# Two transformer-like blocks on images, third stage: the second product runs eleven strips behind the first, its scale is made over three steps, the residual has three buffers, and the loop is written out

## The reference

```python
x = _L0_conv_ref(x, ...)   # shifted 7x7 window attention, then an MLP of 192 hidden units
x = _L1_conv_ref(x, ...)   # the second block:
y = conv7x7_depthwise(x) + dw_b
y = layernorm_over_channels(y)
y = gelu(y @ w1.T + b1)                      # 48 -> 192 features per pixel
gx = sqrt(sum over all pixels of y * y)      # one number per image and feature
nx = gx / (mean of gx over the features + 1e-6)
y = grn_g * (y * nx) + grn_b + y
out = x + (y @ w2.T + b2)                    # 192 -> 48
```

## Time and profile before

| | before |
|---|---|
| runs, us | 2073.83 median of 3 (2071.69 to 2075.19) |
| the profiled execution, us | 2077.34 |
| its span, us | 2075.7 |
| mean granted TensorE clock | 0.946 of full |
| busy: PE, DVE, ACT, POOL | 86%, 73%, 75%, 57% of the span |
| first r_OUT of the response phase starts at | 1734.3 us |
| last r_OUT (strip 63) starts at | 2060.2 us |

### The profile page before, as it was taken

How to read it: one execution, slowest core, us unless ns; L and a number is a source line. 1 busy time by engine, 2 the same in 40 slices (tenths; PEclk the granted TensorE clock), 3 DMA queues, 4 the chain that set the end, 5 groups by cost and what they waited for, 6 DMA issues and landing times. The chain is left out here.

```text
span 2075.7 us, 90932 instructions
## 1 busy us (share of the span) xinstructions
PE 1777.1 (86%) x38074; PEld 1065.6 (51%) x38074; DVE 1508.5 (73%) x2014; ACT 1550.2 (75%) x2882; POOL 1174.7 (57%) x1048
## 2 busy tenths in 40 slices
PE   4989898989888898989898989874999959889884
PEld 2655555555555555555555555531788823223321
DVE  7687777878777777787777777534777757767772
ACT  3788888888888888888888888763566658777770
POOL 4676767777776767676767777731455611111121
PEclk9999999999999999999999999985899957889998
DMA  4334544343434343434434343312587769899983
GB/s 106 80 101 106 146 104 115 91 115 87 119 84 118 86 118 87 109 96 105 100 97 109 93 112 83 93 32 56 155 216 211 203 128 197 218 217 211 242 200 105
DMA packets 233223, 262.18 MB, mean 126 GB/s; under 512 B 167078, under 2 KB 179910, under 8 KB 232710
## 3 DMA queue, kind: packets, MB, share of 16 engines
q1 hardware_dynamic: 217478, 217.50, 43.1%
q0 software_dynamic: 15360, 39.08, 6.6%
HBM read 160.82 MB, written 80.88 MB: 116 GB/s over the span
## 5 line engine op out<-in xcount | busy, mean ns | idle before, releaser
L415 POOL TENSOR_TENSOR shift<-const_b,qmax 113x588 bf16<-113x588 bf16 x256 | 345.8, 1351 | 55.1 <-DVE qmax L510 54.9
L440 POOL TENSOR_TENSOR xl<-x 113x784 bf16<-113x784 f32 x64 | 136.7, 2136 | 263.8 <-DVE x L532 263.8
L1475 POOL DMA_DIRECT2D out_rolled<-r_OUT x128 | 64.3, 504 | 319.5 <-DVE r_OUT L1577 316.4
L510 DVE TENSOR_REDUCE qmax<-ps_s 113x12 f32<-113x588 f32 x256 | 194.7, 760 | 63.0 <-PE ps_s L890 63.0
L496 DVE TENSOR_TENSOR xh<-X,RS 113x784 f32<-113x784 f32 x64 | 229.1, 3580 | 2.9 <-DMA RS<-rs_scratch 2.1
L731 ACT ACTIVATE G<-ps_m 128x392 f32<-128x392 f32 x384 | 184.1, 498 | 50.9 <-PE ps_m L992 50.1
L699 ACT ACTIVATE P<-ps_t 113x588 f32<-113x588 f32 x256 | 171.9, 672 | 54.2 <-PE ps_t L942 53.5
L1323 PE MATMUL conv_ps<-xin,band_now 64*64 64x448 bf16 x2688 | 203.1, 364 | 4.1 <-DVE x_low L1225 4.1
L405 POOL TENSOR_TENSOR xhl<-xh 113x784 bf16<-113x784 f32 x64 | 203.4, 3178 | 2.2 <-DVE xh L550 2.2
L692 ACT COPY Uf<-ps_m 113x392 f32<-113x392 f32 x384 | 172.8, 485 | 30.9 <-PE ps_m L857 22.6
L502 DVE TENSOR_TENSOR Ul<-Uf 113x784 bf16<-113x784 f32 x192 | 182.6, 977 | 0.0
(11 more groups left out here) (240 smaller groups left out, 5267.3 us busy)
## 6 DMA issues: line engine op xcount, KB each, us to landing
xin<-rows_scratch SPq DMA_DIRECT2D x96, 236.0 KB, 3.8
XT<-x_tokens SPq DMA_DIRECT2D x64, 294.0 KB, 4.6
X<-x_windows SPq DMA_DIRECT2D x128, 147.0 KB, 2.9
RS<-rs_scratch SPq DMA_DIRECT2D x128, 147.0 KB, 3.4
XR<-x_windows SPq DMA_DIRECT2D x128, 147.0 KB, 3.7
x_scratch<-x SPq DMA_DIRECT2D x128, 147.0 KB, 3.9
y_scratch<-y POOLq DMA_DIRECT2D x96, 196.0 KB, 2.8
r_RS<-rs_scratch SPq DMA_DIRECT2D x128, 147.0 KB, 3.8
```

Of the source, the lines that this page charges most:

```text
L415: nc.gpsimd.tensor_tensor(shift[:, j % 2], e, m, ALU.mult).then_inc(S["md"], 1)
L440: nc.gpsimd.tensor_tensor(xl1[:], x1[:, r, :], x1m[0][:, r, :], ALU.subtract).then_inc(S["x1_lo"], 1)
L510: nc.vector.tensor_reduce(qmax[:, j % 2, :].rearrange("p (b n) -> p b n", b=2), ps_s[0:R, :, 0:2 * HQ].rearrange("p b (n t) -> p b n t", t ...
```

## The change

The second product, r_OUT and the stores run 11 steps behind the first product in place of 10 (`LAG`), with 14 buffers of features in place of 16 (`RING`); the per-strip sums keep 16 places (`SLOTS`). The making of the scale is taken apart. With B the first step after an image's last strip (strip B-8 is the image's first): in step B, DVE makes r_total, PE adds the halves between its first products of tiles 1 and 2, and ACT takes the square root after the Gelu of tile 2; in step B+1, PE makes the mean of the norms, again between tiles 1 and 2, and ACT (no longer DVE) adds epsilon to it with an Identity and a bias; in step B+2, DVE makes the scale and the scaled weights behind r_OUT; in step B+3, PE uses them. The small products go to spare columns of r_ps_m, and the first product of tile 2 waits until they have been read. On DVE the sum of squares follows its strip by one step in place of two. r_X has three buffers and is loaded one step ahead of its use, at the head of SP's step in place of its end. The hardware loop is gone: all steps are written out.

```diff
--- before.py
+++ after.py
@@ -1377,8 +1377,10 @@
...
         N = strips
-        RING = 2 * STRIPS
-        LAG = STRIPS + 2
+        RING = STRIPS + 6
+        SLOTS = 2 * STRIPS
+        LAG = STRIPS + 3
+        XRING = 3
         by_strip = [t.rearrange("b c (g s n) -> b s g c n", g=2, s=STRIPS) for t in (x2_dram, out_dram)]
@@ -1391,7 +1393,7 @@
...
         Y = sb("r_Y", [R, 2, STRIP])
-        X2 = sb("r_X2", [ROWB + C, 2, STRIP])
+        X2 = sb("r_X2", [ROWB + C, XRING, STRIP])
         OUT = sb("r_OUT", [ROWB + C, 2, STRIP])
@@ -1401,10 +1403,11 @@
...
         junk_act = sb("r_junk_act", [128, 2, STRIP])
-        sums = sb("r_sums", [128, 2, RING])
+        sums = sb("r_sums", [128, 2, SLOTS])
         total = sb("r_total", [128, 2])
...
         mean = sb("r_mean", [128, 1])
+        eps1 = sb("r_eps1", [128, 1])
         inv = sb("r_inv", [128, 1])
@@ -1412,9 +1415,9 @@
...
         S = sems("cleared y_cleared setup_v setup_t f1 f2 pairs mean_ps xh summed summed_act totals "
-                 "gx_made inv_made scaled w2_scaled out_made ge lo")
+                 "gx_made mean_made inv_made scaled w2_scaled out_made ge lo")
         y_loaded = [sem(f"r_y_loaded{r}") for r in range(2)]
-        x2_loaded = [sem(f"r_x2_loaded{r}") for r in range(2)]
+        x2_loaded = [sem(f"r_x2_loaded{r}") for r in range(XRING)]
         stored = [sem(f"r_stored{r}") for r in range(2)]
@@ -1424,16 +1427,9 @@
...
-        def steps(eng, step, last):
-            turns = max((N - RING - 2) // RING, 0)
-            for raw in range(-2, RING):
-                step(Strip(0, raw, N))
-            if turns:
-                with eng.Fori(0, turns) as i:
-                    for u in range(RING):
-                        step(Strip(RING // 4 * i, RING + u, N))
-            for raw in range(RING + RING * turns, last):
+        def steps(step, last):
+            for raw in range(-2, last):
                 step(Strip(0, raw, N))
@@ -1442,7 +1438,15 @@
...
             def step(s):
-                nxt, old = s.at(2), s.at(-LAG)
+                nxt, old = s.at(2), s.at(1 - LAG)
+                if old.real:
+                    if old.n == 0:
+                        wait(sp, S["cleared"], CLEARS)
+                    wait(sp, S["out_made"], old.n - XRING + 1)
+                    for g in range(2):
+                        sp.dma_start(X2[ROWB * g:ROWB * g + C, old.slot(XRING), :],
+                                     by_strip[0][old.n // STRIPS, old.n % STRIPS, g]
+                                     ).then_inc(x2_loaded[old.slot(XRING)], 16)
                 if nxt.real:
@@ -1452,16 +1456,8 @@
...
                                      ).then_inc(y_loaded[r], 16)
-                if old.real:
-                    if isinstance(old.n, int) and old.n == 0:
-                        wait(sp, S["cleared"], CLEARS)
-                    wait(sp, S["out_made"], old.n - 1)
-                    for g in range(2):
-                        sp.dma_start(X2[ROWB * g:ROWB * g + C, old.slot(2), :],
-                                     by_strip[0][old.n // STRIPS, old.n % STRIPS, g]
-                                     ).then_inc(x2_loaded[old.slot(2)], 16)
-            steps(sp, step, N + LAG)
+            steps(step, N + LAG)
@@ -1478,7 +1474,7 @@
...
-            steps(pool, step, N + LAG)
+            steps(step, N + LAG)
             for r in range(2):
@@ -1493,6 +1489,7 @@
...
                 nc.vector.memset(t[:], 1.0).then_inc(S["y_cleared"], 1)
+            nc.vector.memset(eps1[:], EPS1).then_inc(S["y_cleared"], 1)
             dve.wait_ge(S["cleared"], CLEARS)
@@ -1529,19 +1526,17 @@
...
                     wait(dve, S["ge"], 3 * s.n + 3)
-                    g = G[:, s.raw % RING, 2, :]
+                    g, at = G[:, s.raw % RING, 2, :], s.raw % SLOTS
                     wait(dve, S["summed"], s.n)
                     nc.vector.tensor_tensor_reduce(out=junk[:], in0=g, in1=g, scale=1.0, scalar=0.0, op0=ALU.mult,
-                                                   op1=ALU.add, accum_out=sums[:, 1, s.raw % RING:s.raw % RING + 1]
+                                                   op1=ALU.add, accum_out=sums[:, 1, at:at + 1]
                                                    ).then_inc(S["summed"], 1)
-            def image(s):
-                return s.raw // STRIPS if isinstance(s.i, int) else s.i // 2 + s.raw // STRIPS
             def add_up(s):
...
                 if s.real and s.raw % STRIPS == 0:
-                    img, p = image(s), s.raw // STRIPS % 2
+                    img, p = s.raw // STRIPS, s.raw // STRIPS % 2
+                    wait(dve, S["pairs"], img)
                     wait(dve, S["summed"], s.n + STRIPS)
@@ -1550,13 +1545,12 @@
...
                 if s.real and s.raw % STRIPS == 0:
-                    img, p = image(s), s.raw // STRIPS % 2
-                    wait(dve, S["mean_ps"], img + 1)
-                    nc.vector.tensor_scalar(mean[:], ps_o[:, 0, HALF + 2:HALF + 3], EPS1, None, ALU.add
-                                            ).then_inc(S["inv_made"], 1)
-                    wait(dve, S["inv_made"], 2 * img + 1)
+                    img, p = s.raw // STRIPS, s.raw // STRIPS % 2
+                    wait(dve, S["mean_made"], img + 1)
+                    wait(dve, S["scaled"], 2 * img)
                     nc.vector.reciprocal(inv[:], mean[:]).then_inc(S["inv_made"], 1)
-                    wait(dve, S["inv_made"], 2 * img + 2)
+                    wait(dve, S["inv_made"], img + 1)
+                    wait(dve, S["w2_scaled"], 2 * img)
                     nc.vector.scalar_tensor_tensor(out=scale[:], in0=gx[:], scalar=inv[:, 0:1], in1=grn_g[:],
@@ -1571,35 +1565,36 @@
...
                     n = ROWB + C
-                    wait(dve, x2_loaded[s.slot(2)], 32 * (s.turn(2) + 1))
+                    wait(dve, x2_loaded[s.slot(XRING)], 32 * (s.raw // XRING + 1))
                     wait(dve, stored[s.slot(2)], 32 * s.turn(2))
...
                         out=halves(OUT[:, s.slot(2), :]), in0=ps_o[0:n, :, 0:HALF], scalar=out_b[:, 0:1],
-                        in1=halves(X2[:, s.slot(2), :]), op0=ALU.add, op1=ALU.add).then_inc(S["out_made"], 1)
+                        in1=halves(X2[:, s.slot(XRING), :]), op0=ALU.add, op1=ALU.add).then_inc(S["out_made"], 1)
...
                 nx2 = s.at(2)
-                respond(s.at(-LAG))
-                sum_squares(s.at(-2))
-                add_up(s.at(-LAG + 1))
+                sum_squares(s.at(-1))
+                add_up(s.at(-STRIPS))
                 finish(s.at(-LAG))
+                respond(s.at(-STRIPS - 2))
                 normalise(nx2)
-            steps(dve, step, N + LAG)
+            steps(step, N + LAG)
...
             act.wait_ge(S["cleared"], CLEARS)
+            act.wait_ge(S["y_cleared"], 3)
...
                     wait(act, S["summed_act"], s.n)
-                    slot = s.raw % RING
+                    slot, at = s.raw % RING, s.raw % SLOTS
                     nc.scalar.activation(junk_act[:], G[:, slot, 0:2, :], ACT.Square,
-                                         accum_out=sums[:, 0, slot:slot + 1]).then_inc(S["summed_act"], 1)
+                                         accum_out=sums[:, 0, at:at + 1]).then_inc(S["summed_act"], 1)
@@ -1615,18 +1610,30 @@
...
                 if s.real and s.raw % STRIPS == 0:
-                    img = s.raw // STRIPS if isinstance(s.i, int) else s.i // 2 + s.raw // STRIPS
+                    img = s.raw // STRIPS
                     wait(act, S["pairs"], img + 1)
-                    nc.scalar.activation(gx[:], ps_o[:, 0, HALF:HALF + 2], ACT.Sqrt).then_inc(S["gx_made"], 1)
+                    wait(act, S["scaled"], 2 * img)
+                    wait(act, S["mean_ps"], img)
+                    nc.scalar.activation(gx[:], ps_m[:, 0, HALF:HALF + 2], ACT.Sqrt).then_inc(S["gx_made"], 1)
+            def keep_mean(s):
+                if s.real and s.raw % STRIPS == 0:
+                    img = s.raw // STRIPS
+                    wait(act, S["mean_ps"], img + 1)
+                    wait(act, S["inv_made"], img)
+                    nc.scalar.activation(mean[:], ps_m[:, 0, HALF + 2:HALF + 3], ACT.Identity, bias=eps1[:, 0:1]
+                                         ).then_inc(S["mean_made"], 1)
...
                 features(s, 1)
-                norms_root(s.at(-LAG + 1))
                 features(s, 2)
+                keep_mean(s.at(-STRIPS - 1))
+                norms_root(s.at(-STRIPS))
                 sum_squares(s)
-            steps(act, step, N + LAG)
+            steps(step, N + LAG)
@@ -1652,9 +1659,10 @@
...
                         wait(pe, S["lo"], s.n + 1)
-                        wait(pe, S["ge"], 3 * (s.n - 1) + 1)
-                    elif t == 1:
-                        wait(pe, S["ge"], 3 * s.n)
+                    wait(pe, S["ge"], 3 * (s.n - 1) + t + 1)
+                    if t == 2 and s.raw >= STRIPS:
```

(41 more changed lines are left out.)

## The result

The changed kernel takes 2040.1 us (median of 4 runs, 2038.1 to 2042.9) against 2072.8 (median of 4, 2071.4 to 2075.2): ratio 0.984, 95% interval 0.9825 to 0.9859, so 33 us less. The forecast was 2038, 36 less. The profiled execution has a span of 2038.6 us in place of 2075.7.

A forecast was written before the change was run, and what follows sets the result against it. Taken as bounds: r_OUT's waits for r_X and the chain at image boundaries with its low clock. Start +4.9, six images -32.9, end -8.2 sum to -36.2; against 2073.8 that gave 2038 us, range 2026 to 2062.

The forecast's parts named there:

- The residual: Response phase: r_OUT's wait for r_X falls from 36.4 us to under 3; r_Y is late next.
- the tens of us that were to be a sign of being wrong: Sign against the prediction: r_xh waiting for r_Y by tens of us, where it waited 4.6 us before.
- An ordinary strip: Strips between boundaries: 4.16 us at PE's pace where buffers are full, 4.65 in three of eight, 1.5 us an image.
- The boundary: Between two images: 1.0 small products, 1.25 PE waiting for Gelu, 0.7 for the weights; 3.0 us over eight bare strips.
- The clock: TensorE in the response phase: stays up at boundaries, 1.00 through the middle, where a boundary had 0.51.
- The rival with 2.5 us in each image: Clock still falls at each image boundary, costing 2.5 us an image: 2053 us, chance 0.15.
- An image: Eight strips and a boundary: 33.3 + 3.0 + 1.5 = 37.8 us, -32.9 us over six images.
- The start and the end: r_OUT of strip 0 starts 4.9 us later; strips 48 to 63 take 58.1 us, -8.2.
- The loop: All steps written out in place of the hardware loop: 0, bounded at 10 us gained or lost.
- The tables: ACT at boundaries: two loads of 1.28 us without drain, at most 16; rival of Identity needing its own: 2058, chance 0.04.
- PE's pace throughout: Rival, response phase: DMA share over 1 is not full, an image takes 36.3 us: 2029 us, chance 0.12.
- The transfer engines as the bound: Rival: all eight strips at 4.65 us, an image 40.2, +14.4: 2052 us, chance 0.18.

The follow-up runs named there:

- the fastest kernel: Changed kernel with three buffers for r_Y, r_RS and r_OUT, second product ahead of tile 0 except at an image's first strip, scale before sum of squares: 2027.9 us, ratio 0.9771.
- The mixed order: Changed kernel, second product ahead of tile 0 except at an image's first strip, r_OUT and scale before sum of squares: 2033.5 us with two buffers, 2027.9 with three.
- residual alone: Kernel before, loop written out, r_X in three buffers loaded one step ahead at the head of SP's step; lag ten, scale in one step: 2059.1 us, ratio 0.9936.
- four kernels between 2039.6 and 2040.6: Changed kernel 2040.1; from it, r_X loaded for three strips only 2040.3, third buffer for r_Y and r_RS 2040.6, second product first 2039.6 us.

## Why the prediction was right, point by point

*The residual.* Right. Its wait went from 36.4 us to none, r_Y is late next (16.4, short of the tens of us that were to be a sign of being wrong), and the half is worth 15 us alone. What its sum priced nowhere is that a wait for r_X may cost clock too. In the trace before, r_OUT of one ordinary strip waited 3.29 us for r_X, the second product behind it 2.55, and the low level began 0.7 us after PE resumed:

```profile
1810.20 1.03 DVE L1577 SCALAR_TENSOR_TENSOR r_OUT<-r_ps_o,r_out_b,r_X 112x784 f32<-112x784 f32 x1 [3.29 <-DMA r_X<-x_scratch]
1811.29 2.23 PE L1700 MATMUL r_ps_o<-r_G,r_w2s_own 128*64 128x392 f32 x8 [2.55 <-DVE r_OUT L1577]
```

*An ordinary strip.* The mechanism was right, its second price not. The prediction let three of eight strips run at 4.65, for the transfers. In the image from strip 16 (1815.93) to strip 24 (1853.20), 37.27 us, none did: all stand at 4.15. That term was 1.5 us an image too much. The 265 GB/s behind it are no limit, as the prediction itself allowed: the fastest kernel moved 277 over 100 us.

*The boundary.* Too cheap: 3.0 forecast, 4.0 measured in that same image (37.27 less 8 x 4.15): 1.55 in step B, 2.03 in B+1, 0.45 in B+3. The step that failed is the one that charged step B with the halves' adding alone (0.5). PE also stands 0.94 there for r_total, as r_Y, late, holds DVE; in the kernel without residual loads, where r_Y is in time, step B costs 0.54. The other terms came near what was worked out: 1.44 for Gelu behind the table loads (forecast 1.25), 0.45 for the weights (0.7).

*The clock.* The low level did not return at each boundary, but in two images of six (3.4 and 6.8 us at 1.2 GHz, which cost some 4 us, 0.7 an image). That, with step B at 5.3 on the average, makes the mean image 37.6 and the boundary 4.4. The forecast of 1.00 through the middle was thus a little high: it is 0.98. The rival with 2.5 us in each image is refuted for this kernel, but it was near: in the kernels without residual loads and with the second product first the low level came in five images of six.

*An image.* 37.8 forecast, 37.6 measured: the strips' 1.5 too much and the boundary's 1.0 to 1.4 too little cancelled. The total was right partly by luck.

*The start and the end.* +4.9 forecast, +4.0 from the phase's first product on; the other 2.1 of strip 0's delay came from the untouched phases, and differs from profile to profile (the first first-product stands at 1689.1 to 1693.4 in these kernels). -8.2 forecast, -8.9 measured.

*The loop.* Priced at 0 and measured at 0. One reading beside it is wrong and carries nothing: the slices before the response phase are not all at full clock, three of them show 8, 5 and 8 tenths.

*The tables.* Sixteen loads in the phase, and Identity needed none. By line, from 1690 to 2026:

```profile
L1608 ACT ACT_TABLE_LOAD x8 | 10.3, 1283 | 19.3 <-PE r_ps_f L1678 19.2
L1617 ACT ACT_TABLE_LOAD x8 | 10.3, 1283 | 0.1
L1625 ACT ACTIVATE r_mean<-r_ps_m,r_eps 128x1 f32<-128x1 f32 x8 | 2.2, 274 | 2.8 <-PE r_ps_m L1698 2.8
```

Gelu starts at 1844.37, 0.01 after the end of the load that began at 1843.08, and the load itself begins within 0.02 of the end of the instruction before it. The drain of about 1380 ns that the Trainium skill gives in ScalarE: Activation LUTs (What ACT_TABLE_LOAD costs) is on neither side; the measurement decides, and the prediction was right to go by its row.

*The other rivals.* PE's pace throughout was right on the strips and wrong on the boundary (3.0 there, 4.4 measured). The transfer engines as the bound is refuted by the strips at 4.15 and by the kernels with third buffers, which move every byte in an image of 36.2 and 35.2 us. That all transfers share the same 16 engines and interleave (the Trainium skill, DMA: Bandwidth & Descriptors, Issuing engines are not separate DMA queues) agrees with the times to landing: 5.4 us for r_Y with the residual's loads beside it, 3.9 without. An earlier issue bought lead, and lead was what was short.

What stays open: a correct root by way of another engine, without table loads, was not tried; the run without it bounds its worth in this order at 9.7 us. Nor is it shown why the same stop of 1.44 us lets the clock fall in some images and not in others, nor how often it does so from one execution to the next.

## What to carry to other kernels

Before pricing a freed wait, list every stop of PE in the same period and ask which will take its place. The three single changes that gave nothing failed in three ways: the clock fell at the stop that stayed (no residual loads), another tile's two buffers ran short (third buffer for r_Y), the stop moved to the next link of the chain (second product first). The mixed order gave 6.6 us alone and 12.2 with three buffers of r_Y, r_RS and r_OUT. When a load is late, add a buffer to separate lead from rate: if the wait goes while all bytes still move, rate was not the bound. Taking bytes out can't tell them apart, as it also makes the loads land sooner. A chain across engines that stands between two periods can be spread over the steps behind it, one link a step, with each link placed behind work that has to be done anyway: here that took an image's boundary from 6.8 us (residual alone: 40.0 less eight strips of 4.15) to 4.4.

## What the hardware showed that was not expected

In the profiled executions, a stop taken away made another one dearer: without the residual's loads, the same 1.44 us of PE's waiting came with 3.4 to 6.8 us at 1.2 GHz in five images of six instead of two, and four kernels between 2039.6 and 2040.6 differ in their waits and not in their time. A DMA share above 1 was no ceiling: 265 GB/s at 1.06 before, 277 GB/s at 1.07 in the fastest kernel, where PE was busy 95.2 of 100 us. More buffers raised the time of a transfer more than the rate: a third buffer for r_Y and r_RS took r_Y's time to landing from 5.4 to 6.7 us, while the six images' window moved 252 GB/s in place of 254.
